# Placing the source block of the table by a SyncE transfer inside SBUF instead of a GpSimd copy

## The reference, cut to what matters

```python
# gated network (twice): ei of the source, ej and h of the destination
gate = silu(edge_attr @ F1W + F1b) @ F2W + F2b
gate = gate + (emb[atom_z[src]] * (emb[atom_z[dst]] @ adapt)).sum(-1, keepdims=True)
msg = gate * h[dst] * (cw * node_mult[dst])[:, None]
agg = segment_sum(msg, src, N)
# attention, L = 4 layers
score = (Q[src] * K[dst]).sum(-1) + 0.1 * (edge_attr * Q[src][:, :40]).sum(-1) + logm[dst]
alpha = softmax of score over the edges of each src
aggi = segment_sum(alpha[:, None] * (h[dst] @ Wm[i]), src, N)
```

## Time and profile before

| what | value |
|---|---|
| median of 3 executions | 14100.42 us |
| profiled execution, its own time | 14074.54 us |
| its span | 14072.9 us |
| busy: TensorE, VectorE, ScalarE, GpSimd | 11362.4 (81%), 12048.1 (86%), 8518.8 (61%), 7253.3 (52%) us |
| `source_block` copies on GpSimd, 1560 | 257 to 721 ns, median 320 |
| strips in stages with a source side | 6 x 260 |

### The profile page before, as it was taken

The page is one execution under the profiler, slowest core; times in us unless marked ns, Lnnn a source line. Parts: engine busy times, 40 slices in busy tenths (PEclk is TensorE's granted clock), DMA queues, the critical chain, the costliest instruction groups (busy, mean ns, idle before and its releaser), DMA issues.

```text
span 14072.9 us, 633514 instructions
## 1 busy us (share of the span) xinstructions
PE 11362.4 (81%) x194575; PEld 9684.0 (69%) x194575; DVE 12048.1 (86%) x29590; ACT 8518.8 (61%) x28750; POOL 7253.3 (52%) x9217
## 2 busy tenths in 40 slices
PE   2899999976666899888998889888996667586566
PEld 2566666856666877787777877787776666576566
DVE  5788888487898899888998899888998889699997
ACT  0566666174676788768886788768885212067630
POOL 0577777463454555355553555355552455565436
PEclk9999999998656755595556755595555678685597
DMA  9433333765996877577774877577776967489857
GB/s 378 129 85 85 85 85 85 34 190 192 280 286 210 269 190 190 143 282 200 190 190 163 272 189 191 148 277 204 193 193 193 293 198 224 134 304 282 241 196 205
DMA packets 3519118, 2771.39 MB, mean 197 GB/s; under 512 B 2341145, under 2 KB 3123096, under 8 KB 3518730
## 3 DMA queue, kind: packets, MB, share of 16 engines
q1 hardware_dynamic: 2793658, 1085.99, 30.7%
q0 software_dynamic: 236192, 860.68, 21.0%
q10 hardware_dynamic: 489008, 821.78, 15.7%
HBM read 1655.83 MB, written 1111.61 MB: 197 GB/s over the span
## 4 chain that ended last, share of the span: by engine, by line
PE 26%; DVE 24%; DMA 14%; issue 14%; ACT 11%; DVEq 5%; SPq 4%; ACTq 2%; POOL 1%; POOLq 0%
DMA chunk_layer_rows<-arena 7%; DVE arena L1916 6%; PE ps L1190 5%; ACT arena L1051 5%; PE ps L1181 4%; DMA arena<-edge_hot_b 3%; DVE arena L1843 3%; PE ps L1337 3%; PE ps L1304 2%; PE ps L1173 2%; DVEq L110 2%; PE ps L1210 2%; DVE arena L1821 2%; PE ps L1372 1%; DMA chunk_gated<-arena 1%
## 5 line engine op out<-in xcount | busy, mean ns | idle before, releaser
L1337 PE MATMUL ps<-arena 128*128 128x49 bf16 x56160 | 2586.6, 213 | 894.7 <-DVE arena L1859 425.5
L1337 PEld LDWEIGHTS ps<-arena 128*128 128x128 fp8e4 x56160 | 2328.3, 115 | 1205.8 <-issue 1194.2
L1304 PE MATMUL ps<-block_tables,arena 128*128 128x98 bf16 (+2 forms) x56160 | 2444.7, 200 | 603.0 <-DVE arena L1829 318.3
L1304 PEld LDWEIGHTS ps<-block_tables,arena 128*128 128x128 bf16 (+1 forms) x56160 | 2213.8, 99 | 834.3 <-issue 422.3
L763 POOL COPY block_tables<-arena 128x294 bf16 (+2 forms) x2340 | 1428.9, 611 | 2220.4 <-PE ps L1304 1306.2
L987 ACT ACTIVATE arena<-ps 128x392 f32<-128x392 f32 (+1 forms) x3900 | 1710.4, 480 | 1041.5 <-PE ps L1304 639.3
L725 POOL DMA_INDIRECT edge_records<-arena x1563 | 1610.6, 1030 | 959.7 <-issue 509.5
L747 POOL DMA_INDIRECT arena<-chunk_layer_rows,map_a x1040 | 1041.7, 1002 | 2020.6 <-ACT arena L1051 1930.9
L1051 ACT ACTIVATE arena<-arena,small 128x49 f32<-128x49 f32 x8320 | 1997.2, 323 | 101.7
L1829 DVE TENSOR_SCALAR arena<-arena,iota_row 128x1024 bf16<-128x1024 uint8 x2080 | 1565.7, 753 | 113.0 <-PE ps L1304 56.2
L1916 DVE CUSTOM_DVE_ANT_0 arena<-ps,arena 128x1024 bf16<-128x1024 f32 x1040 | 1273.3, 1224 | 335.7 <-PE ps L1372 225.2
(11 more groups left out here) (327 smaller groups left out, 20355.7 us busy)
## 6 DMA issues: line engine op xcount, KB each, us to landing
chunk_layer_rows<-arena ACTq DMA_DIRECT2D x1040, 392.0 KB, 3.3
arena<-node_hot_a SPq DMA_DIRECT2D x1820, 128.0 KB
arena<-edge_hot_a SPq DMA_DIRECT2D x1560, 128.0 KB
chunk_gated<-arena ACTq DMA_DIRECT2D x520, 324.0 KB, 2.6
arena<-edge_records SPq DMA_DIRECT2D x1040, 160.0 KB
chunk_rows<-arena ACTq DMA_DIRECT2D x780, 196.0 KB, 1.9
arena<-edge_records SPq DMA_DIRECT2D x520, 196.0 KB
arena<-edge_hot_b SPq DMA_DIRECT2D x780, 128.0 KB
```

Source lines behind the costliest of these rows:

```text
L1304: last = pe.matmul(psv[:, 2 * r + j // tpb, (j % tpb) * w:(j % tpb + 1) * w], hot[:, s, j * P:(j + 1) * P], bt4[:, s, i, 0:w], start=i == ...
L1337: last = pe.matmul(to[s % 2], he4j[:, s % 4, j, :], low_part(i, s, j), start=j == 0 and i == 0, stop=j == C8 - 1 and i == 2)
```

## The change

The GpSimd copy, its register read and the semaphore `st_made` go. In its place SyncE, between the node hots and the edge records of a strip, reads the block's number and issues a transfer from `tab_s` to the strip's place in `src_tab`, both in SBUF: 128 rows of 300 bytes. It adds to the same semaphore as the node hots, so TensorE and ScalarE wait for both with one count (`hots_landed`: 32 for each use of a place instead of 16; the stage in which hots alone are loaded counts 16). SyncE is held before these stages until the table is ready; GpSimd's own wait for that before attention goes. GpSimd's key addition stays four strips behind its gather. The places now receive all of a table block's 3 x 50 columns, so VectorE clears `tab_s` once in the prologue (3675 words a partition).

```diff
+            def place_source(k, s, b):
+                sp.dma_start(src_tab[:, s % 4 * 3 * TSW:(s % 4 + 1) * 3 * TSW],
+                             tab_s[:, bass.ds(b * (3 * TSW), 3 * TSW)]).then_inc(ht_loaded[s % 4], 16)
+            SP_BLOCKS = (mybir.EngineType.SP, blk_a)
...
             def layer(l):
                 spread(l + 1, row_b)
-                walk(nc, sp, NS, [(0, load_node_hots(l * 2 + 3, l)), (0, load_edges(0, R, at["keys"], l * NS)), (2, load_edge_hots(hot_ea, l + 1))])
+                hold(sp, "sp", (table_ready, l * 2 + 3))
+                walk(nc, sp, NS, [(0, load_node_hots(l * 2 + 3, l)), (0, place_source, True), (0, load_edges(0, R, at["keys"], l * NS)),
+                                  (2, load_edge_hots(hot_ea, l + 1))], SP_BLOCKS)
...
-            def source_block(w, used, base, k):
-                _, regs = nc.values_load_multi_w_load_instructions(
-                    blk_a[0:1, k:k + 1], engines=(mybir.EngineType.Pool,), min_val=0, max_val=NB - 1,
-                    skip_runtime_bounds_check_because="VectorE clamps it")
-                if k >= 4:
-                    pool.wait_ge(used, base + k - 3)
-                of = tab_s[:, bass.ds(regs[0] * (3 * TSW), 3 * TSW)].rearrange("p (i c) -> p i c", c=TSW)
-                pool.tensor_copy(st4[:, k % 4, :, 0:w], of[:, :, 0:w]).then_inc(st_made, 1)
...
-                pool.wait_ge(table_ready, l * 2 + 3)
-                collect(ed_l, ROWL, at["ph"], l * NS, WK, at["q"], l * NS, lambda k: keys(l, k))
+                gather(ed_l, ROWL, map_a, at["ph"], l * NS, after=lambda k: keys(l, k - 4) if k >= 4 else None)
+                for k in range(NS - 4, NS):
+                    keys(l, k)
...
             def hot_there(hl, k, s):
-                pe.wait_ge(ht_loaded[s % 4], landed(hl, k, s, 4))
+                pe.wait_ge(ht_loaded[s % 4], hots_landed(hl, k, s))
...
                     hot_there(l + 1, k, s)
-                    pe.wait_ge(st_made, (l + 1) * NS + k + 1)
...
             dve.sem_inc(angle_ready, 1)
+            do(dve.memset(tab_s.bitcast(F32), 0.0))
             do(dve.memset(z[:, :], 0.0))
```

More of the change, by code:

```diff
@@ L490, in landed, with hots_landed, hots_alone_landed @@
             return (pass_no * (NS // ring) + 1) * 16 + (k - s % ring) * (16 // ring)
+        def hots_landed(hl, k, s):
+            s = s % 4
+            alone = NS // 4 * 16 if isinstance(hl, int) and hl == HT_G2 else 0
+            return hl * (NS // 4) * 32 + (k - s) * 8 + 32 - alone
+        def hots_alone_landed(k, s):
+            return HT_C1 * (NS // 4) * 32 + 16 + (k - s) * 4
         def rows_landed(hm_no, k, s):
@@ L663, in _ @@
             spread(HM_G1, row_b)
-            walk(nc, sp, NS, [(0, load_node_hots(KB_G1 + 1)), (0, load_edges(G1_0, WK, gt["msg"], 0)), (2, load_edge_hots(hot_ea, 0, KB_G1 + 1))])
+            hold(sp, "sp", (table_ready, 1))
+            walk(nc, sp, NS, [(0, load_node_hots(KB_G1 + 1)), (0, place_source, True), (0, load_edges(G1_0, WK, gt["msg"], 0)),
+                              (2, load_edge_hots(hot_ea, 0, KB_G1 + 1))], SP_BLOCKS)
             sp.wait_ge(gt["msg"], NS)
@@ L682, in _ @@
             sp.wait_ge(at["keys"], L * NS)
-            walk(nc, sp, NS, [(0, load_node_hots(KB_G2 + 1)), (0, load_edges(G2_0, WK, gt["msg"], NS)), (2, load_edge_hots(hot_ea, HS_G2))])
+            hold(sp, "sp", (table_ready, 2 * L + 4))
+            walk(nc, sp, NS, [(0, load_node_hots(KB_G2 + 1)), (0, place_source, True), (0, load_edges(G2_0, WK, gt["msg"], NS)),
+                              (2, load_edge_hots(hot_ea, HS_G2))], SP_BLOCKS)
             spread(HM_C3, row_a)
@@ L765, in stage_blocks @@
                 walk(nc, pool, NS, [(0, copy, True)], (mybir.EngineType.Pool, blk))
-            def source_block(w, used, base, k):
-                _, regs = nc.values_load_multi_w_load_instructions(
-                    blk_a[0:1, k:k + 1], engines=(mybir.EngineType.Pool,), min_val=0, max_val=NB - 1,
-                    skip_runtime_bounds_check_because="VectorE clamps it")
-                if k >= 4:
-                    pool.wait_ge(used, base + k - 3)
-                of = tab_s[:, bass.ds(regs[0] * (3 * TSW), 3 * TSW)].rearrange("p (i c) -> p i c", c=TSW)
-                pool.tensor_copy(st4[:, k % 4, :, 0:w], of[:, :, 0:w]).then_inc(st_made, 1)
[L777 to L788, removed]
             stage_blocks(0, KB_G1, WG, blk_b, 1)
             spread_stored(0)
-            collect(ed_g, ROWG, gt["mj"], 0, G, ht_used, (KB_G1 + 1) * NS)
+            gather(ed_g, ROWG, map_a, gt["mj"], 0)
             def keys(l, k):
@@ L819, in _ @@
             spread_stored(SP_G2)
-            collect(ed_g, ROWG, gt["mj"], NS, G, ht_used, (KB_G2 + 1) * NS)
+            gather(ed_g, ROWG, map_a, gt["mj"], NS)
             stage_blocks(SP_C3, KB_C3, WK, blk_a, 2 * L + 5)
@@ L1310, in hot_there, with pick_src @@
             def hot_there(hl, k, s):
-                pe.wait_ge(ht_loaded[s % 4], landed(hl, k, s, 4))
-            def pick_src(hl, st_no, w, bank, free, base):
+                pe.wait_ge(ht_loaded[s % 4], hots_landed(hl, k, s))
+            def pick_src(hl, w, bank, free, base):
                 def step(k, s):
```

13 lines of the change are left out of this document (6 added, 7 removed).

## The result

The kernel with the change takes 14320.41 us (median of 4, 14305.81 to 14341.71), the kernel before 14102.44 us (median of 4 on the same chip). The ratio is 1.0155, 95% interval 1.0137 to 1.0172: slower, by 218 us. The forecast was 14238 us, the range 14100 to 14350.

The account below looks back on a forecast made before the run. VectorE was taken to bound the gated stages, attention alternating between VectorE, ScalarE and issue; SyncE would become the gated bound. Gated +179, collisions -30, starts -15, memset +4 sum to +138 on the profiled execution: 14238 us on the median, range 14100 to 14350.

Parts of the forecast that it names:

- SyncE already works 2.24 and 2.36 us of a strip of 2.8, and 0.5 us are free.: Gated stages: SyncE waits only 0.54 and 0.45 us a strip, so added work makes it the bound, +179 us.
- 0.94 us a placement: SyncE's added work per strip in all six stages: 0.19 preparation, 0.33 issue, 0.42 register read with its steps.
- Nearest row: Pricing SyncE's new transfer at 0.33 us, from the trace's issue of 128 rows.
- Some relief for stretched issues, 0.1: Gated stages: a slower pace shortens SyncE's stretched issues, taking 0.1 us off a strip, to 3.08 and 3.20.
- Collisions: -30 of up to -99: Attention: VectorE's subtractions stop colliding with GpSimd's copy, 0.095 us a strip; 30% taken as on the path, -30 us.
- The keys' addition: Attention: GpSimd's remaining addition could take the copy's place in collisions, but records issued 0.9 us later would move it.
- Attention hides the placement: Attention: SyncE waits 1.96 us a strip, so the added 0.94 fits and the landing is hidden by 1.2; cost 0.
- Stage starts, -15: Starts of six stages: the first source block arrives 2.5 us earlier in each, -15 us.
- Memset, +4: Prologue: VectorE clears the table, 3.1 us plus 1.05 idle, +4 us.
- the queue does not bind: Rival, gated stages: SyncE's added work disappears in its stretched issues and costs nothing, total 14059 us; chance 0.13.
- the dear register read: Rival, gated stages: SyncE's register read costs GpSimd's 0.562 us, 135 us more, total 14373; chance 0.10.

Follow-up runs that it names:

- experiment 4: The changed kernel with the gated stages' edge hots issued by ScalarE instead of SyncE: 15619.3 us, ratio 1.0026 to the kernel before.
- experiment 3: The changed kernel with SyncE always placing block 0 in the gated stages, without a register read: 15673.2 us, ratio 1.0043 to the kernel before.
- experiment 2: The changed kernel with GpSimd's copy back in attention, SyncE placing only in the gated stages: 15898.8 us, ratio 1.0187 to the kernel before.
- experiment 7: The kernel before, with GpSimd copying one column of each part from attention's fifth strip on: 15521.7 us, ratio 0.9945.
- experiment 9: SyncE placing in attention only, with GpSimd's old copy also made there into a spare buffer: 15638.8 us, ratio 1.0034 to the kernel before.
- experiment 12: The kernel before, with GpSimd's copy moving the same bytes as 32-bit words, plus the table memset: 14062.6 us, ratio 0.9975.
- experiment 5: The kernel before, unchanged, run again on one of the slower chips: 15570.8 us, ratio 0.9997.
- experiment 6: The changed kernel, unchanged, run again on one of the slower chips: 15887.0 us, ratio 1.0205 to the kernel before.
- experiment 1: The changed kernel with GpSimd's copy back in the gated stages, SyncE placing only in attention: 15619.0 us, ratio 1.0015 to the kernel before.
- experiment 10: SyncE placing in attention only, issued last, behind the edge records and edge hots: 15655.1 us, ratio 1.0043 to the kernel before.

## Why the prediction was right, and where its sum was off

It forecast slower because SyncE becomes the bound of the gated stages. That is what happened; it was 82 us short of the median. Against the profiled executions it was 104 short (+138 for +242): 141 too little in the gated stages and 17 in what lies around them, less 47 in attention and 8 at the stage starts. The profiled execution of before lay 26 us under the runs' median, that of after 4. That the median fell into the range is in part luck: with the gated stages at their +320 and the rest as forecast the sum is 14100 + 320 - 30 - 15 + 4 = 14379, above the range's 14350, and attention's larger gain brought it back.

- *SyncE already works 2.24 and 2.36 us of a strip of 2.8, and 0.5 us are free.* Right: its waits vanish, the chain runs mostly through it, and taking one issue from it (experiment 4) gives 140 of the added 163 and 160 us back. VectorE's idle time was foreseen behind TensorE's source query (50.9 us in the window above); more of it stands behind the landing of the records (65.6), which SyncE issues last but one.
- *0.94 us a placement.* This is the term that was mis-sized. The chain shows 1.16; experiments 3 and 2 give 0.78 - 0.19 + 0.46 = 1.05. All but the issue was about right (1.16 - 0.53 = 0.63 where 0.61 was forecast, the read 0.278 for 0.30). The issue was taken at 0.33, the price of 128 rows from DRAM, but 128 rows from SBUF to SBUF take 0.528. With 1.16 the prediction's own sum gives 2.24 + 1.16 - 0.1 = 3.30 and 3.42 us a strip; measured are 3.36 and 3.44. "Nearest row" was chosen by the number of rows alone, and the 0.55 of the edge records was the other row at hand. That the address from a register is not the reason is shown by experiment 3; whether it is the source in SBUF or the rows of 300 bytes, no run separates.
- *Some relief for stretched issues, 0.1.* About right for the sum, though the records' issue became longer, 0.60 instead of 0.56.
- *Collisions: -30 of up to -99.* The mechanism was right, the size too small on the chip of the comparison: the subtractions fell from 609 and 606 to 564 and 567, 0.084 us a strip, and 77 / 1040 = 0.074 us came off the path, which is most of it and not 30%. A third line that the sum left out fell too, the low part of the maximum (L1929), from 191 to 152 ns, while a neighbour, L1911, grew from 168 to 183; all of VectorE's lines together lost 0.09 us a strip (910.02 us in 230 strips, 908.65 in 235). Taking the line's share of the chain of waits for the part of its length that counts was the step that failed here. The copy's part is shown by experiments 7, 9 and 12, that the path is VectorE's only on chips like that of the comparison by experiments 5 and 6. The Trainium skill, page "SBUF — State Buffer", section "Who interferes with whom", names this pair, a VectorE instruction with two SBUF inputs and a GpSimd instruction that reads SBUF. These runs agree: the first subtraction takes 604 ns with the copy (experiment 9) and 566 without it (experiment 1), the operation with PSUM 564 in both. The keys' addition did not take the copy's place; as foreseen it now waits for its records (3.03 us at the start of the stage, 274.6 us in the 1000 us window where it waited 35.8).
- *Attention hides the placement.* Right on the chip of the comparison. On the others the stages gain nothing although the collisions vanish, and the one-column copy gains 21 to 26 us a stage. It is not the order of the issues (experiment 10), and not a full SyncE (it waits 0.89 us a strip). The chain runs through TensorE there (52%, and 79% with the placement), and VectorE waits for it. But the one-column copy shows that TensorE can go through a stage in 1137 us there; why it takes 1157 beside the placement stays open.
- *Stage starts, -15.* The sum was -23, but from another place: nothing in attention, where SyncE's hold for the table cost what the gathers had, and 11 to 12 us in each gated stage.
- *Memset, +4.* Right: 3.12 us and 0.94 idle.

```profile
3196.56 3.12 DVE L1690 MEMSET arena<- 128x3675 f32 x1 [0.94 <-DVE log_mult L1688]
```

- *The rivals.* That the queue does not bind is out by experiments 2 and 4, the dear register read by its row: 0.278 at the median. The Trainium skill, page "DMA: Bandwidth & Descriptors", section "Latency and other measured facts", gives about 600 ns as the floor of such a load; the shortest here is 263 ns, so the measurement decides against it.

## What to carry to other kernels

Before work is moved to an engine that only issues transfers, count its strip: pace less its waits is what it works already, and the rest is all there is to give. Price an issue by a row of the same kind (source and destination, not only the rows it moves), and add the register read and the steps between. Two issues of the same kind can still differ: node hots and edge hots are both 128 rows of 1 KB from DRAM, and their medians are 0.346 and 0.439 us in the changed kernel. Where two engines collide in SBUF, making the smaller one's instruction shorter (fewer, wider elements) gave 0.25% (interval 0.15 to 0.34), while moving it away in all six stages cost 1.5%. Moving it where there is room, in attention alone, gained nothing on two of the slower chips and was not run on one of the others.

## What the runs showed that was not expected

An issue by SyncE costs by its kind, in medians of the changed kernel: 0.35 us for the node hots and 0.44 for the edge hots, both 128 rows of 1 KB from DRAM to SBUF, 0.53 for 128 rows of 300 bytes within SBUF, 0.60 for 1024 pieces of records. A register read costs SyncE 0.278 us.

The same program does not run at the same pace on each chip, whatever the granted clock in the rows says. Windows of 1000 us in the prologue, where TensorE is the busy one: the kernel before and the changed one in the first comparison, then the kernel before on one of the slower chips (TensorE's busy time and count first, the granted clock third from the end):

```profile
1000.00:2000.00 1000.00, 999.65 (x5623) 688.07 (x5623) 851.99 (x1997) 616.43 (x2539) 746.35 (x726) 1.00 0.32 85
```

```profile
1000.00:2000.00 1000.00, 999.62 (x5623) 687.99 (x5623) 852.82 (x1997) 617.04 (x2539) 749.32 (x727) 0.50 0.33 85
```

```profile
1000.00:2000.00 1000.00, 700.60 (x3919) 479.33 (x3920) 587.87 (x1397) 436.65 (x1778) 501.11 (x506) 0.50 0.22 59
```

5623 matmuls at a granted clock of 1.00 (2.4 GHz) and again 5623 at 0.50 (1.2 GHz), but 3919 at 0.50 on the other chip. The first two lines say that the recorded halving cost nothing there; the third that on some chips the same stretch runs 1.43 times longer with the same record. By the rows a single matmul takes no longer there (999.65 / 5623 and 700.60 / 3919 are both 178 to 179 ns); what grew is waiting. The page of that run has it:

```profile
L1608 DVE TENSOR_TENSOR arena<-ps,arena 128x392 f32<-128x392 f32 x391 | 220.9, 565 | 997.7 <-remote 901.3
```

Of the 1.1 ms by which the prologue is longer, VectorE stands idle for 901 us before this line, waiting for something that the trace only calls "remote"; between 1000 and 2000 us it does so 42 times, for up to 8.2 us. By the code it waits there for a count that TensorE raises, whose matmuls by their rows have ended up to 8 us before. The ends of matmuls are modelled, so a TensorE that stalls for some microseconds would look like this, but no run shows what it is. A comparison across chips would have been worth nothing here, and even a ratio on one chip (attention's -77 us or 0) need not carry over to the next.
